# Cross attention on one core: bias products in three row groups, one GQA shift and exponential, separate softmax buffers, and new engine orders

## The chip, the cores and the metric

The kernel runs on one core of one Trainium2 chip. The time is that of the whole program on the device in microseconds. TensorE multiplies matrices, VectorE (DVE), ScalarE (ACT) and GpSimd (POOL) compute elementwise, SyncE (SP) issues the DMAs. Results of products land in PSUM, which here has eight banks of 512 float32 columns.

## The reference, cut to what matters

64 sequences `x` (128 tokens of width 128), each with a context of 77 tokens of width 256, pass through four cross attention layers. Layers 0 and 2 are grouped-query (GQA: 16 query heads of width 8, 4 key heads, RMS norm ahead), layers 1 and 3 are multi-head (MHA: 16 heads of width 64) with a bias on the score columns of four tokens.

```python
# layers 0 and 2
q = (rmsnorm(x, norm_w) @ wq).reshape(B, T, 16, 8)
k, v = [(cond @ w).reshape(B, S, 4, 8) for w in (wk, wv)]
attn = softmax(einsum('btgrd,bsgd->bgrts', qg, k) / sqrt(8))
x = x + einsum('bgrts,bsgd->btgrd', attn, v).reshape(B, T, 128) @ wo
# layers 1 and 3
logits = einsum('bhqd,bhkd->bhqk', x @ Wq, ctx @ Wk) / 8
col_bias[:, token_indices_A] = (-20 * (1 - mask_A))[:, None]
col_bias[:, token_indices_B] = (-20 * (1 - mask_B))[:, None]
probs = softmax(logits + col_bias)
x = x + einsum('bhqk,bhkd->bqhd', probs, ctx @ Wv) @ Wo + bo
```

## The kernel before

An item is one layer of one sequence. Eight sequences (streams) are under way at once, and `ITEMS` lists their 32 items so that GQA and MHA items alternate; `j` is an item's place. The loop body is `pair(it, n)`, written once for each engine: it handles GQA item g = 2n and MHA item m = 2n + 1, and, as a pipeline, parts of items before and after them (g + 2, g + 4, m - 2, m - 4, m - 6). The order of the calls in these five functions is the order of the engine's instructions; semaphores named after values tie the engines together, and `at(name, it, j, k)` gives the count to wait for. Pairs run 128 times, with some empty ones ahead (from n = -3, the fill) and behind (the tail).

Float32 accuracy is had from float16 products in three passes: a value is split into a high part (ScalarE, `high`) and a low part (VectorE `low`, or GpSimd `low_part`), and hi*hi, hi*lo, lo*hi are added in PSUM (`split_product`). For MHA, Wk and Wq are folded ahead of the loop into `m_w`; in the loop `folded` makes `g_s`, the keys seen from x, in six chunks for two streams at a time, three chunks a pair.

One item's scores are 16 heads x 77 keys = 1232 columns in `sc`, three PSUM banks of 512, 512 and 208 columns. Per MHA item, `scores_m(it, m, k)` fills bank k: first a bias product (L1350: `bias_l` times `bias_r`, both of 128 rows of which the first six are not zero), then three score products onto it (L1352). It waits for `sg_sub` or `sm_sub`, by which the shift of the item before has read the bank. Then `maximum_m` and `shift_m` on VectorE take the row maximum off into `shifted`, `exponential_m` on ScalarE writes `probs`, `high_m` and `low_part` split it into `p_sm`, and `turn_m` on SP transposes that by DMA into `p_tm`. `values_m` multiplies with the values, `normalise_m` and `normalise_rest` divide by the denominators, `high_out` and `low_out` split the result, `turn_out` transposes it, `output_m` multiplies with Wo, and `finish_m` adds the residual, or in layer 3 `last_layer` copies it to `y_out`, which `store` writes out. GQA items go the same way (`scores_g`, `maximum_g`, `shift_g` in two halves of 539 and 693 columns, `exponential_g` and `high_g` in two halves of 512 and 720, `values_g`, `normalise_g`, `rest_and_turn`, `turned`, `output_g`, `finish_g`); their keys are spread into `k_bd` by `spread_keys` on GpSimd, and their values are brought to packed form by `pick_values`, `picked_values` and `pack_values`. `probs` and `shifted` are one buffer each for both kinds; `item_before` says whose reading has to be over.

All other products take turns in `ring`, three PSUM banks. `ring_uses(n)` lists a pair's uses in TensorE's order, `bank_for` gives the bank and waits until the use three places before has been read.

`bias_factors` prepares `bias_l` and `bias_r` ahead of the loop on VectorE; each of its steps waits for the one before.

## Time and profile before

| | us |
|---|---|
| median of 3 runs | 1851.74 |
| lowest, highest | 1850.95, 1852.22 |
| profiled execution | 1852.7 |
| its span on the core | 1850.9 |
| TensorE busy in it | 1792.3 (97%) |
| VectorE, ScalarE, GpSimd busy | 1593.3 (86%), 1471.6 (80%), 1507.8 (81%) |
| TensorE's mean granted clock | 0.977 of full speed |

The page divides the span into 40 slices: TensorE stands at 9 tenths or more from the third to the last but one, and its granted clock at 9 tenths or more there too. A product's busy time covers its way through the array and into PSUM, so that successive products overlap in it; the cost of one in a stream is the distance from its start to the next start. In the timeline rows a group's first number is the start of its first instruction.

### The profile page before, as it was taken

The page shows a single profiled execution, that of the slowest core. Times are in us where ns is not written, and L with a number is a line of the kernel's source. Part 1 is how long each engine was busy: PE and PEld are TensorE (multiplying, and loading weights), DVE is VectorE, ACT ScalarE, POOL GpSimd, SP SyncE. Part 2 cuts the span into 40 slices and gives each one's busy share as a digit, 9 for nine tenths or more (in the row PEclk, how much of TensorE's full clock was granted, in tenths as well). Part 3 has the DMA queues.
Part 4 walks back from the last instruction along what each step waited for, and adds up shares of the span by engine and source line. Part 5 has one row for each costly group of instructions (what it writes and reads, how often), then busy time and mean ns, then how long its engine had stood idle before and what let it go on. Part 6 is the DMA issues. An engine that isn't in the chain of part 4 may idle for free.

```text
span 1850.9 us, 72762 instructions
## 1 busy us (share of the span) xinstructions
PE 1792.3 (97%) x28272; PEld 1557.7 (84%) x28272; DVE 1593.3 (86%) x3130; ACT 1471.6 (80%) x2859; POOL 1507.8 (81%) x1880
## 2 busy tenths in 40 slices
PE   6699999999999999999999999999999999999995
PEld 6578888888888888888888888888888888888884
DVE  6589988889888998898888998889888988889973
ACT  4378888888888888888888888888888888888872
POOL 3388888888888888888888888888888888888873
PEclk7599999999999999999999999999999999999998
DMA  5279999999999899999999999999899999989995
GB/s 170 42 140 183 167 187 183 184 182 166 178 192 180 181 168 184 185 173 188 175 180 187 177 175 178 182 190 177 176 178 186 185 173 177 169 176 178 177 165 128
DMA packets 1168210, 320.36 MB, mean 173 GB/s; under 512 B 1140246, under 2 KB 1164124, under 8 KB 1167868
## 3 DMA queue, kind: packets, MB, share of 16 engines
q1 hardware_dynamic: 1167868, 315.69, 93.1%
q8 instruction: 228, 3.74, 0.9%
q14 instruction: 114, 0.93, 0.2%
HBM read 15.93 MB, written 4.19 MB: 11 GB/s over the span
## 4 chain that ended last, share of the span: by engine, by line
PE 92%; issue 1%; DMA 0%; DVE 0%; POOL 0%; SPq 0%; ACT 0%
PE ring L1215 48%; PE sc L1352 11%; PE o_ps L1215 9%; PE o_ps L1370 5%; PE ring L1424 5%; PE sc L1335 4%; PE sc L1350 4%; PE ring L1286 2%; PE ring L1410 1%; PE ring L1405 1%; PE ring L1421 1%; PE sc L1327 1%; PE ring L1263 0%; PE o_ps L1366 0%; PE ring L1266 0%
## 5 line engine op out<-in xcount | busy, mean ns | idle before, releaser
L1215 PE MATMUL ring<-ctx_four,m_w 128*128 128x154 f16 x6144 | 441.4, 230 | 1.5 <-DVE v_tile L915 0.9
L1215 PEld LDWEIGHTS ring<-ctx_four,m_w 128*128 128x128 f16 x6144 | 422.8, 96 | 1.9 <-DVE v_tile L915 1.1
L636 POOL TENSOR_TENSOR p_sg<-arena,p_sg 128x512 f16<-128x512 f32 (+1 forms) x256 | 347.4, 1357 | 89.8 <-ACT p_sg L702 89.8
L1092 DVE TENSOR_TENSOR arena<-sc,row_max 128x616 f32<-128x616 f32 (+2 forms) x512 | 402.6, 797 | 13.2
L641 POOL TENSOR_TENSOR p_sm<-arena,p_sm 128x616 f16<-128x616 f32 x256 | 334.1, 1319 | 4.4 <-ACT p_sm L702 2.5
L664 POOL TENSOR_TENSOR arena<-arena 128x1024 f16<-128x1024 f32 x128 | 273.4, 2136 | 40.5 <-ACT arena L702 40.4
L702 ACT ACTIVATE arena<-ring 128x462 f16<-128x462 f32 (+1 forms) x384 | 198.3, 516 | 133.8 <-PE ring L1215 132.5
L1215 PE MATMUL ring<-wv_m,ctx_four 128*103 128x512 f16 (+1 forms) x1152 | 281.2, 380 | 0.6 <-DVE q_mix L919 0.6
L1071 DVE TENSOR_TENSOR arena<-ring,arena 128x462 f16<-128x462 f32 (+1 forms) x384 | 223.8, 584 | 64.2 <-ACT arena L702 55.4
L1352 PE MATMUL sc<-arena,x_s 128*128 128x512 f16 (+1 forms) x1152 | 262.2, 336 | 0.0
L1089 DVE TENSOR_REDUCE row_max<-sc 128x6 f32<-128x462 f32 (+2 forms) x384 | 223.7, 583 | 44.2 <-PE sc L1352 38.8
L812 ACT ACTIVATE arena<-arena,log_w,rstd 128x512 f32<-128x512 f32 (+1 forms) x256 | 228.3, 892 | 9.5 <-DVE arena L1092 9.5
L827 ACT ACTIVATE arena<-arena,log_w 128x616 f32<-128x616 f32 x256 | 204.0, 797 | 6.6 <-POOL p_sg L636 4.6
L702 ACT ACTIVATE v_tile<-ring 103x512 f16<-103x512 f32 (+1 forms) x192 | 114.9, 598 | 106.8 <-PE ring L1215 102.8
L1215 PEld LDWEIGHTS ring<-wv_m,ctx_four 128*103 128x103 f16 (+1 forms) x1152 | 136.3, 127 | 69.3 <-DVE q_mix L919 0.8
L702 ACT ACTIVATE p_sm<-arena 128x616 f16<-128x616 f32 x256 | 183.6, 717 | 6.1
L702 ACT ACTIVATE p_sg<-arena 128x512 f16<-128x512 f32 (+1 forms) x256 | 182.6, 713 | 4.1
L1084 DVE TENSOR_REDUCE row_max<-sc 128x16 f32<-128x1232 f32 x128 | 183.1, 1430 | 0.0
L1352 PEld LDWEIGHTS sc<-arena,x_s 128*128 128x128 f16 x1152 | 109.9, 97 | 76.3
L607 POOL TENSOR_TENSOR x_sq<-x_f 128x128 f32<-128x128 f32 x128 | 51.5, 402 | 146.6 <-ACT x_f L702 146.6
L915 DVE SCALAR_TENSOR_TENSOR v_tile<-ring,v_tile 103x512 f16<-103x512 f32 (+1 forms) x192 | 132.2, 689 | 40.9 <-ACT v_tile L702 40.9
L1141 DVE TENSOR_TENSOR arena<-o_ps,den_r 128x896 f32<-128x896 f32 x128 | 139.7, 1091 | 4.4
(165 smaller groups left out, 3797.4 us busy)
## 6 DMA issues: line engine op xcount, KB each, us to landing
v_fourth<-v_tile SPq DMA_DIRECT2D x64, 105.6 KB
ctx_nat<-in_ctx_dram SPq DMA_DIRECT2D x64, 77.0 KB
x_nat<-in_x_dram SPq DMA_DIRECT2D x64, 64.0 KB, 2.4
arena<-p_sg SPq DMA_TRANSPOSE x256, 3.9
arena<-p_sm SPq DMA_TRANSPOSE x256, 4.1
out_dram<-y_out SPq DMA_DIRECT2D x64, 64.0 KB, 2.1
v_fourth<-v_tile SPq DMA_DIRECT2D x32, 101.6 KB
arena<-in_L_xattn_Wk_dram SPq DMA_DIRECT2D x2, 1024.0 KB, 6.1
```

The lines of the kernel that those rows point to most:

```text
L636: pool.tensor_tensor(p_sg[k][:, LO, 0:e - a], probs_flat[:, a:e], p_sg[k][:, HI, 0:e - a], ALU.subtract).then_inc(sems["pg_lo"], 1)
L641: pool.tensor_tensor(p_sm[:, k, LO, :, 0:S], probs[:, hs, :], p_sm[:, k, HI, :, 0:S], ALU.subtract).then_inc(sems["pm_lo"], 1)
L664: pool.tensor_tensor(o_s[:, LO, :], o_n, o_s[:, HI, :], ALU.subtract).then_inc(sems["o_lo"], 1)
L702: return act.activation(out, in_, ACT.Copy, scale=scale)
L812: act.activation(probs_flat[:, a:e], shifted_flat[:, a:e], ACT.Exp, bias=log_w[:, :], scale=rstd[:, r:r + 1]).then_inc(sems["pg_exp"], 1)
L827: act.activation(probs[:, hs, :], shifted[:, hs, :], ACT.Exp, bias=log_w[:, :], scale=MHA_SCALE).then_inc(sems["pm_exp"], 1)
L1071: dve.tensor_tensor(both[LO], ring[:, b, 0:(h1 - h0) * 2 * S].rearrange("p (h t s) -> p h t s", t=2, s=S), both[HI], ALU.subtract).then_in ...
L1084: dve.tensor_reduce(row_max[:, :], s_view, AX_X, ALU.max).then_inc(sems["sg_max"], 1)
L1089: dve.tensor_reduce(row_max[:, h0:h1], s_view[:, h0:h1, :], AX_X, ALU.max).then_inc(sems["sm_max"], 1)
L1092: dve.tensor_tensor(shifted[:, hs, :], s_view[:, hs, :], row_max[:, hs].unsqueeze(2).to_broadcast([P, hs.stop - hs.start, S]), ALU.subtrac ...
L1215: ins = pe.matmul(out, a, b, start=(n == 0), stop=(n == len(passes) - 1))
L1352: ins = pe.matmul(sc_flat[:, a:e], x_s[st][:, x, :], g[:, y, a:e], start=False, stop=(x == LO))
```

## The change

- **Bias products.** `bias_factors` copies the six bias rows of `bias_l` and `bias_r` to partitions 32 and 64 too. `scores_m` issues all three bias products at k = 0, bank b from rows 32b to 32b + 5, and the score products follow; it waits once for both halves of the shift before.
- **GQA shift and exponential** are one operation each of 1232 columns. `high_g` keeps its two parts.
- **Buffers.** `probs_g`, `shifted_g`, `probs_m`, `shifted_m` replace `probs` and `shifted`; the waits go by item two places before, of the same kind. `x_sq` has three buffers and not eight.
- **Orders.** All five `pair` functions and `ring_uses` are written in a new order.

```diff
+        return [("vp", g - 2, 0), ("ot", g - 4, 0), ("g", lead, chunks[0]), ("ym", m - 6, 0), ("g", lead, chunks[1]),
+                ("kv", g + 2, 0), ("g", lead, chunks[2]), ("yg", g - 4, 0), *[("ct", g + 4, 0)] * (layer(g + 4) == 0 or n % PAIRS == CT_EXTRA), ("q", g + 2, 0),
+                *[("v", j, k) for j, k in value_chunks(n)[0:1]], *[("v", j, k) for j, k in value_chunks(n)[1:2]]]
...
-        probs = in_arena(HS, F32).rearrange("p (h s) -> p h s", s=S)
-        shifted = in_arena(HS, F32).rearrange("p (h s) -> p h s", s=S)
+        probs_g, shifted_g = in_arena(HS, F32), in_arena(HS, F32)
+        probs_m, shifted_m = [in_arena(HS, F32).rearrange("p (h s) -> p h s", s=S) for n in range(2)]
...
+                for k in range(1, 3):
+                    step(dve.tensor_copy(bias_l[32 * k:32 * k + 6, :], bias_l[0:6, :]))
+                    for n in range(2):
+                        step(dve.tensor_copy(bias_r[n][32 * k:32 * k + 6, :, :], bias_r[n][0:6, :, :]))
...
+            def shift_g(it, g):
                 dve.wait_ge(sems["sg_max"], at("sg_max", it, g, 1))
-                shifted_free(it, g, k)
-                shift(G_SUB[k], sems["sg_sub"])
+                if exists(it, g - 2):
+                    dve.wait_ge(sems["pg_exp"], at("pg_exp", it, g - 2, 1))
+                shift(shifted_g.rearrange("p (h s) -> p h s", s=S), slice(0, H), sems["sg_sub"])
...
-                scores_free(it, m, min(k, 1) + 1)
-                ind = bias_r[w][:, :, :].rearrange("p h s -> p (h s)")
                 a, e = k * BANK, min(HS, (k + 1) * BANK)
-                pe.matmul(sc_flat[:, a:e], bias_l[:, :], ind[:, a:e], start=True, stop=False)
+                if k == 0:
+
+                    scores_free(it, m, 2)
+                    ind = bias_r[w][:, :, :].rearrange("p h s -> p (h s)")
+                    for b in range(3):
+                        c0, c1, rows = b * BANK, min(HS, (b + 1) * BANK), slice(32 * b, 32 * b + 6)
+                        pe.matmul(sc_flat[:, c0:c1], bias_l[rows, :], ind[rows, c0:c1], start=True, stop=False)
```

The new order of TensorE is: `pick_values(g - 2)`, `values_m(m - 4)`, `rest_and_turn(g - 4)`, `scores_g(g)`, first folding chunk, `output_m(m - 6)`, second chunk, `keys_values(g + 2)`, third chunk, `scores_m` 0 and 1, `output_g(g - 4)`, `turn_inputs(g + 4)`, `queries(g + 2)`, `scores_m` 2, `values_g(g - 2)`, the context values. On GpSimd `spread_keys(g + 2)` now stands ahead of the low parts of item g; `pack_values` is a pair later and right behind `low_out`. On ScalarE `turned(g - 4)`, `high_out(m - 4)` and `last_layer(m - 6)` stand behind the first folding chunk, `keys_values` ahead of the exponential, `picked_values` behind the second value chunk. On SP both halves of `turn_m(m)` are in pair n, with `turn_out(m - 2)` behind them.

The three places below show what stands in a row on an engine. Behind each instruction are the semaphores that it waits for.

TensorE, in the middle of the run, from the keys and values of a GQA item (`wk_r`, `wv_g`) through the MHA scores (`sc<-arena,x_s`) to the last bank's scores; before:

```order
L1215 MATMUL ring<-wv_g,ctx_four 77x48 x6
L1350 MATMUL sc<-bias_r,bias_l 128x512 [waits sg_sub,g_lo,xm_lo]
L1352 MATMUL sc<-arena,x_s 128x512 x3
L1350 MATMUL sc<-bias_r,bias_l 128x512 [waits sg_sub,g_lo]
...
L1215 MATMUL ring<-x_s,wq_r 128x128 x11
L1350 MATMUL sc<-bias_r,bias_l 128x208 [waits sg_sub,g_lo]
L1352 MATMUL sc<-arena,x_s 128x208 x3
```

and after:

```order
L1206 MATMUL ring<-ctx_four,m_w 128x154 x11
L1345 MATMUL sc<-bias_r,bias_l 128x512 [waits sg_sub,g_lo,xm_lo]
L1345 MATMUL sc<-bias_r,bias_l 128x512
L1345 MATMUL sc<-bias_r,bias_l 128x208
L1347 MATMUL sc<-arena,x_s 128x512 x3
L1347 MATMUL sc<-arena,x_s 128x512 [waits g_lo]
L1347 MATMUL sc<-arena,x_s 128x512 x2
L1405 MATMUL ring<-o_tg,wo_g 128x128 [waits ot_copy,g_lo]
```

The second and third bias product moved up to the first, and the folding's last chunk (`m_w`) stands ahead of them where keys and values stood.

VectorE, around the GQA maximum (`row_max<-sc 128x16`) and shift, in the middle of the run; before:

```order
L1141 TENSOR_TENSOR arena<-o_ps,den_r 128x896 [waits om_rcp]
L1137 RECIPROCAL den_r<-ring 128x2 [waits om_norm,ot_raw,om_raw]
L1083 TENSOR_SCALAR ms<-sc 128x1 [waits sg_raw]
L1084 TENSOR_REDUCE row_max<-sc 128x16
L1092 TENSOR_TENSOR arena<-sc,row_max 128x539 [waits pm_exp,sg_max]
L1092 TENSOR_TENSOR arena<-sc,row_max 128x693 [waits pm_exp,sg_max]
```

and after:

```order
L1131 TENSOR_TENSOR arena<-o_ps,den_r 128x896 [waits om_rcp]
L1127 RECIPROCAL den_r<-ring 128x2 [waits om_norm,ot_raw,om_raw]
L1077 TENSOR_SCALAR ms<-sc 128x1 [waits sg_raw]
L1078 TENSOR_REDUCE row_max<-sc 128x16
L1065 TENSOR_TENSOR arena<-ring,arena 128x3x2x77 [waits g_hi]
L1086 TENSOR_TENSOR arena<-sc,row_max 128x1232 [waits pg_exp,sg_max]
L1065 TENSOR_TENSOR arena<-ring,arena 128x3x2x77 [waits g_hi]
```

The shift is one instruction and has a folding low part (L1065) ahead of it.

ScalarE, the last instructions of the program; `arena<-arena 128x1024` is `high_out`, `y_out` is `last_layer`, `arena<-ring,den_r` is `normalise_rest`; before:

```order
L702 ACTIVATE y_out<-ring 128x128 [waits stored5,ym_raw]
L702 ACTIVATE arena<-arena 128x1024 [waits turned_o,om_norm]
L745 ACTIVATE arena<-ring,den_r 128x64 [waits om_norm,om_rcp]
L745 ACTIVATE arena<-ring,den_r 128x64
L702 ACTIVATE y_out<-ring 128x128 [waits stored6,ym_raw]
...
L702 ACTIVATE y_out<-ring 128x128 [waits stored7,ym_raw]
```

and after:

```order
L698 ACTIVATE arena<-arena 128x1024 [waits turned_o,om_norm]
L698 ACTIVATE y_out<-ring 128x128 [waits stored5,ym_raw]
L741 ACTIVATE arena<-ring,den_r 128x64 [waits om_norm,om_rcp]
L741 ACTIVATE arena<-ring,den_r 128x64
...
L698 ACTIVATE y_out<-ring 128x128 [waits stored6,ym_raw]
L698 ACTIVATE y_out<-ring 128x128 [waits stored7,ym_raw]
```

Each `high_out` moved ahead of the `y_out` of the MHA item before.

## Rows read from the trace of the kernel before

**Rows 1.** Busy time by stretch: stretch, length, busy of each engine, PEclk, DMA share, GB/s

```profile
500.00:1000.00 500.00, 499.97 (x8067) 434.56 (x8067) 444.64 (x863) 417.54 (x817) 427.99 (x529) 1.00 0.99 181
1012.00:1015.00 3.00, 3.00 (x36) 2.21 (x35) 2.71 (x5) 2.55 (x4) 2.42 (x2) 1.00 1.27 280
```

**Rows 2.** TensorE's waits (us, times, longest): longest of 100 to 1800, one of the fill

```profile
PE ring L1215 <- DVE v_tile L915: 0.9, 1, 0.9
...
PE sc L1335 <- POOL k_bd L650: 6.0, 2, 3.4
```

**Rows 3.** Timeline of TensorE in one pair: start, us, engine, line, operation, count

```profile
1004.08 0.35 PE L1215 MATMUL ring<-v_tile,arena 128*128 128x65 f16 x6
...
1005.08 1.50 PE L1215 MATMUL ring<-arena,wo_m 128*128 128x128 f16 x24
1006.42 3.40 PE L1215 MATMUL ring<-ctx_four,m_w 128*128 128x154 f16 x48
1009.66 0.22 PE L1366 MATMUL o_ps<-zeros,arena 128*128 128x144 f16 x1
...
1010.48 0.38 PE L1215 MATMUL ring<-ctx_four,wk_r 128*128 128x77 f16 x6
...
1010.91 0.38 PE L1350 MATMUL sc<-bias_r,bias_l 128*128 128x512 bf16 x1
1011.13 0.81 PE L1352 MATMUL sc<-arena,x_s 128*128 128x512 f16 x3
```

**Rows 4.** Timeline of TensorE ahead of the loop, products of 64 rows

```profile
39.29 4.68 PE L1242 MATMUL sc<-arena 64*128 64x128 f32 x21
...
43.94 0.42 PE L1242 MATMUL ring<-arena 64*128 64x128 f32 x1
43.98 0.41 PE L1242 MATMUL sc<-arena 64*128 64x128 f32 x1
```

**Rows 5.** Groups by shape (busy us, mean ns): bias product, its weight load

```profile
L1350 PE MATMUL sc<-bias_r,bias_l 128*128 128x512 bf16 x256 | 96.9, 378 | 0.0
...
L1350 PEld LDWEIGHTS sc<-bias_r,bias_l 128*128 128x128 bf16 x384 | 38.0, 99 | 15.6
```

**Rows 6.** Timeline of VectorE in the pair of rows 3

```profile
1003.25 1.09 DVE L1141 TENSOR_TENSOR arena<-o_ps,den_r 128x896 f32<-128x896 f32 x1
...
1005.83 1.43 DVE L1084 TENSOR_REDUCE row_max<-sc 128x16 f32<-128x1232 f32 x1
...
1008.13 0.87 DVE L1092 TENSOR_TENSOR arena<-sc,row_max 128x693 f32<-128x693 f32 x1
1008.92 1.89 DVE L1071 TENSOR_TENSOR arena<-ring,arena 128x462 f16<-128x462 f32 x3
```

**Rows 7.** Timeline ahead of the loop: a bias_r copy, TensorE's first product of the loop

```profile
38.85 0.79 DVE L1003 CAST bias_r<-arena 6x1232 bf16<-6x1232 f32 x1
...
55.34 0.48 PE L1263 MATMUL ring<-ident,x_nat 128*128 128x128 f32 x1 [4.58 <-DVE m_w L915]
```

**Rows 8.** Timeline of the fill: the two operands of one item's scores

```profile
79.87 0.75 DVE L919 SCALAR_TENSOR_TENSOR q_mix<-q_hi,minus_low,ring 128x512 f16<-128x512 f16 x1 [2.32 <-ACT q_hi L702]
...
81.24 0.70 POOL L650 TENSOR_TENSOR k_bd<-k_mix,group_mask 128x308 f16<-128x308 f16 x1
```

**Rows 9.** Timeline of the tail: y_out, last rest product, both transposes, last high_out

```profile
1827.09 0.28 ACT L702 ACTIVATE y_out<-ring 128x128 f32<-128x128 f32 x1 [4.36 <-PE ring L1424]
...
1828.74 0.35 PE L1215 MATMUL ring<-v_fourth,arena 128*128 128x65 f16 x6
...
1830.69 1.58 SPq L518 DMA_TRANSPOSE arena<-arena  x1
...
1837.96 1.05 ACT L702 ACTIVATE arena<-arena 128x1024 f16<-128x1024 f32 x1
...
1841.41 1.51 SPq L518 DMA_TRANSPOSE arena<-arena  x1
```

More of the change, by code:

```diff
@@ L350, in build @@
         x_s = [sb(f"x_s{n}", [P, 2, T], F16) for n in range(STREAMS)]
-        x_sq = [sb(f"x_sq{n}", [P, T], F32) for n in range(STREAMS)]
+        x_sq = [sb(f"x_sq{n}", [P, T], F32) for n in range(3)] * 3
         y_out = [sb(f"y_out{n}", [P, D], F32) for n in range(STREAMS)]
@@ L544, in pair @@
                     turn_g(it, g, 1)
+                if exists(it, m - 2) and part(m - 2) != 3:
+                    move_values(it, m - 2)
                 if exists(it, m):
                     turn_m(it, m, 0)
+                    turn_m(it, m, 1)
+                if exists(it, m - 2):
+                    turn_out(it, m - 2)
                 if layer(g + 4) == 0 and exists(it, g + 4) and exists(it + 1, g + 4):
@@ L686, in pair @@
                 if exists(it, m):
-                    low_part(it, m, 0)
                     low_part(it, m, 1)
+                if layer(g + 4) == 0 and part(g + 4) == 3 and exists(it, g + 4):
+                    context_parts(it, g + 4)
             for n in range(-3, PAIRS):
@@ L1452, in pair @@
                     scores_m(it, m, 2)
+                if exists(it, g - 2):
+                    values_g(it, g - 2)
                 for j, k in value_chunks(n)[0:1]:
@@ L1475 @@
 CONSTS = 21
-ARENA = 15232
+ARENA = 16256
 SMALL_LOADS = 20
-DVE_STEPS = 73
+DVE_STEPS = 79
 _GQA = ("wq", "wk", "wv", "wo", "norm_w")
```

186 lines of the change are left out of this document (83 added, 103 removed).

## The prediction

> **What bounds the kernel now.** I read the busy table by stretches first. In the 500 us from 500 to 1000 TensorE is busy for 499.97 us at the full granted clock (1.00, the 2.4 GHz level), VectorE for 444.6, ScalarE for 417.5, GpSimd for 428.0 [rows 1]. A busy TensorE could still hide short waits, since the ends of its matmuls are modelled, so the waits of TensorE between 100 and 1800 us come next: the longest is 0.9 us, and there are three in all, 2.1 us together [rows 2]. In the middle of the run the time is therefore the sum of what TensorE issues, and only work taken off TensorE shortens it. The DMA share of 0.99 looks like a second ceiling but is none: in 3 us of backlog the same queue shows a share of 1.27 at 280 GB/s, against 181 GB/s on average [rows 1], so it has a third in hand. The ends of the run are different: there TensorE waits, 6.0 us of it in the fill for `k_bd` alone [rows 2].
>
> **The bias products.** Today each of the 128 MHA items issues three of them, in a chain with the score products. Starts in the timeline give their price: 1010.91 to 1011.13 is 0.22 us for one of 512 columns (there are two such) [rows 3], and the one of 208 is 0.09 at the same rate. Together 0.53 us an item. After the change the three stand in a row and read six rows each, at partitions 0, 32 and 64, into three different banks. Whether products in different row groups run at once is shown by the weight folding at the start, whose products have 64 rows and stand in one group or the other: 21 of them in a row last 4.68 us, the last one 0.41 of it, so they start 0.21 us apart, while where the groups alternate one starts at 43.94 and the next at 43.98 [rows 4]. So they do run side by side, and what is left is the longest, 0.22, and 0.01 to 0.04 for the later starts (0.04 is the gap of those rows; I take 0.01, since the second of a pair waits there for its own group): 0.23. Gross gain 0.30 us an item, 38 us in all.
>
> Against that stands what no row of the trace shows: the change from full-height products to six-row ones and back, twice an item. From below it costs nothing. From above, TensorE would let the pipeline run out and load weights in the open each time: a product of 512 columns lasts 0.378 us but its successor starts after 0.22, so 0.16 us of it is normally covered, and a weight load of that line lasts 0.10 [rows 5]. Twice 0.26 is 0.52 us an item, and the change would then lose 0.22 us. I take 0.11 us an item, a third of the two covered ends and no open load: waiting for the array alone is a part of those 0.16 us (the rest is reading and writing), and nearly every weight load of the trace lies under other work. That leaves 0.19 us an item, **minus 24.3 us**. Here the Trainium skill speaks against the change: its page "TensorEngine Tiling (Array Packing)", section "Key Properties", says that changing the tiling mode drains TensorE. No row of this trace shows it. Its page "TensorE: Matmul & The Clock Gate", section "Measured speedup vs the span model", gives 3.07 times for four row groups at 512 columns, which as an estimate from that page is some 280 ns a set and a gain of some 0.25 us an item, or 32 us, if the switches are in it.
>
> **The new order in the middle.** No work is added to TensorE, so the order costs something only if a producer becomes late. The tightest place is the first bias product: it writes all three banks, so it now waits for the whole GQA shift, and the shift is one operation. From the last score product of the GQA item (end near 1005.08) to the first of the MHA item TensorE issues the output product (1005.08 to 1006.42), the folding (to 1009.66) and keys and values (1010.48 to 1010.91), 1.34 + 3.24 + 0.43 = 5.01 us [rows 3]; `values_g`, which stood there too, moves behind and takes 0.82 us of cover with it. VectorE has to do in that time the maximum 1.43, one folding low part (a third of 1.89), a short residual sum (0.3 at most) and the shift, now 128x1232 (0.87 for 693 columns, so 1.5) [rows 6]: 3.9 us. Ahead of that it has `normalise_m`, 1.09 and two short reciprocals, about 1.5 us, which waits for `values_m`; that ends 1.0 us before the scores do (1004.08 to 1005.08, the small rest product and the scores) [rows 3], so VectorE comes some 0.5 us late. 0.5 + 3.9 = 4.4 against 5.0: 0.6 us in hand. The second tight place is the `ot` bank, freed by ScalarE's `turned` behind its first folding copy: two short copies under the output product's 1.34 us, with some 0.4 in hand. `values_m`, although the code now names m - 4, stands at nearly the same place of the stream, so the transposes keep the cover they have. Work on the other engines shrinks a little (one shift and one exponential in place of two), and separate buffers only take waits away. GpSimd's `low_out` stands ahead of `pack_values` now, and `values_g` is late enough for it. I put **0** for all this; what it costs if the cover is gone is the second rival. Two small exceptions are at the ends.
>
> **The start.** `bias_factors` gets six more copies, each waited for. VectorE is busy without a gap there, and TensorE's first product of the loop at 55.34 waits 4.58 us for VectorE's last weight part [rows 7], so they count in full. A copy of 6x1232 from float32 took 0.79 [rows 7]; four from bf16 at 0.4 to 0.8 and two narrow ones at 0.25: 2.1 to 3.7, **plus 2.9**.
>
> **The fill.** `spread_keys` leaves its place behind both low parts on GpSimd. The second `k_bd` came at 81.24 + 0.70 = 81.94, while the other operand of the same scores, `q_mix`, was there at 79.87 + 0.75 = 80.62 [rows 8]. What is late next is `q_mix`, which also loses the copy of the picked values ahead of it (0.5 us on ScalarE). So of the 6.0 us about half comes back: **minus 3** (bounds 0 and minus 6).
>
> **The tail.** Before, ScalarE's `high_out` of an item stands behind the last copy `y_out` of the item before: high_out of the last item starts at 1837.96, right behind that copy, and after GpSimd's low part its transpose goes out at 1841.41, 3.45 us on [rows 9]. After, `high_out` stands ahead of `y_out`, and the transpose waits only for the output product of the item before, its single buffer. For the last but one item that was over when y_out began at 1827.09; its transpose went out at 1830.69 [rows 9], so it comes 3.6 us sooner. Its output product, over before 1837.96, is then over before 1834.4. The last item's own values end at 1828.74 + 0.35 = 1829.1 [rows 9]; normalising takes about 1.6 and the rest on ScalarE 0.5, and 3.45 more bring 1834.6. The last transpose leaves there and not at 1841.41: **minus 7** (bounds minus 3 and minus 9, as the clock falls here and there).
>
> **The sum.** Minus 24.3 + 2.9 - 3 - 7 = minus 31.4 us. The profiled execution took 1852.7 us (span 1850.9), 1 us over the median of 1851.7, so 1821.3 by its own time and **1820.5** as a median. A measurement of this kernel can tell about 0.2%, 3.7 us, from no change.
>
> **The rivals.** First, the slower side: **the switches cost more than the side by side run saves**. It decides at 0.30 us an item from where the bias products stop paying, and at 0.30 + 7.1/128 = 0.36 from where the kernel is slower; at the full 0.52 the bias alone adds 28 us and the time is 1852.7 + 28 - 7 - 1 = 1873. For it speaks that this stream never lets TensorE run dry and six-row products come in the middle of it; against it, that three quarters or more of both open ends would have to be paid. I give 0.10. The page on tiling named above would be right about the drain in either case; only its size decides.
>
> Second, **the new order starves TensorE**: the shift of 1232 columns, or `ot_copy`, is late by more than the 0.4 to 0.6 us in hand, in every pair. Each 0.1 us of it costs 12.8 us, 0.24 us eat the whole gain, and a stall of 0.3 us gives 1821 + 38 = 1859. For it: VectorE is 89% busy [rows 1], and the chain through it is now a closed one of few steps. Against it: the 11% left over are more than it needs, and it waits for TensorE in each pair, so that it can't fall behind slowly. Chance 0.09.
>
> Third, **the three products don't overlap**, for instance because their weight loads or starts follow one another: the bias stays at 0.53 us and only the ends pay, 1852.7 - 7 - 1 = 1844.6. The alternating starts of [rows 4] speak against it. Chance 0.06.
>
> **How the numbers follow.** The forecast, with its bias gain between 0 and 38 us, has 0.75. Its ends are 1852.7 - 38 - 1 - 7 - 5 = 1802 (full overlap, free switches, a better fill and tail) and about 1847. The range reaches from 1802 to 1851: it takes in the third rival and leaves out the first two for the most part and 0.03 below, 0.17 in all. Faster by over 0.2% (below 1848): 0.75 + 0.06, less the thin upper end and plus the mild cases of the first two, 0.82. Within 0.2%: 0.05. Slower: 0.13.
>
> **What would show it.** In the profile after, the starts of the first bias product and of the score product behind it should lie 0.30 to 0.38 us apart, where 0.53 went in three pieces before; 0.23 means free switches, 0.53 or more the first or third rival, and the starts of the three tell which (a few ns apart or 0.2 us). A full-height product just ahead of the first would show the switch in. TensorE's waits from 100 to 1800 should stay near 2 us; a line `sc <- DVE` on the bias line or `ring <- ACT o_tg` with over a hundred entries is the second rival. The first product of the loop should start near 58 in place of 55.34, the `k_bd` line should lose most of its 6.0 us, and the last two output products should start about 7 us apart, not 11. I would be wrong most likely in the price of the switch, next in the ends.

## The result: two thirds of the bias products' gain is paid back in changes of height

The changed kernel took **1838.8 us** in the median (1836.3 to 1839.6, 4 runs) beside 1852.0 (1851.0 to 1853.3) for the kernel before on the same chip: ratio 0.9926, 95% interval 0.9909 to 0.9943. Measured again (experiment 9), it gave 1837.9 (1837.3 to 1840.1) against 1854.3, ratio 0.9915 (0.9901 to 0.9928). So it is faster by 13.2 to 16.5 us, where 31 were forecast: the sign and the range held, the size was about twice too large. Three executions at a lower mean granted clock (0.65 to 0.84) are left out of all medians: 2538.3 and 2024.3 us of the kernel before, and 2211.8 us of experiment 2. The profiled execution took 1836.3 us (span 1834.5), the fastest of its four; against the profiled one of before it is 16.4 us shorter.

First, is TensorE still what bounds the middle? The busy table of that stretch (stretch, length, busy of TensorE, its weight loads, VectorE, ScalarE, GpSimd, then the granted clock, DMA share, GB/s), answering to [rows 1]:

```profile
500.00:1000.00 500.00, 500.00 (x8116) 430.32 (x8114) 442.11 (x831) 402.53 (x783) 427.86 (x532) 1.00 0.98 182
```

And its waits from 100 to 1785 us (total, times, longest), then three of those between 55 and 110 us, answering to [rows 2]:

```profile
PE ring L1206 <- ACT o_tg L698: 1.6, 2, 0.8
PE ring L1206 <- DVE v_tile L905: 0.3, 1, 0.3
```

```profile
PE ring L1254 <- DVE m_w L905: 6.8, 1, 6.8
PE ring L1254 <- DVE v_gqa L905: 6.2, 3, 2.6
PE sc L1326 <- DVE q_mix L909: 2.0, 2, 1.2
```

In the middle nothing is waited for: the same full clock, 1.9 us of waits in all. There the time is still the sum of what TensorE issues, and whatever is missing of the gain lies in TensorE's own stream. In the fill the `k_bd` line of [rows 2] is gone, but others have come. The timeline of TensorE around one MHA item's first scores (start, us, line, operation, count), answering to [rows 3]:

```profile
1004.28 0.38 PE L1206 MATMUL ring<-wv_g,ctx_four 128*77 128x48 f16 x6
1004.50 0.97 PE L1206 MATMUL ring<-ctx_four,m_w 128*128 128x154 f16 x12
1005.41 0.39 PE L1345 MATMUL sc<-bias_r,bias_l 6*128 6x512 bf16 x3
1005.73 1.47 PE L1347 MATMUL sc<-arena,x_s 128*128 128x512 f16 x6
1007.03 0.38 PE L1405 MATMUL ring<-o_tg,wo_g 128*128 128x128 f32 x2
```

The three bias products last 0.39 us together, one product's length: they do run at once. From the first's start to the score product is 1005.73 - 1005.41 = 0.32 us. Single products at the same place show what the group's row hides, the distance in front of it. TensorE's products, then the loads of the bias weights, then the score products behind the first:

```profile
1005.25 0.23 PE L1206 MATMUL ring<-ctx_four,m_w 128*128 128x154 f16 x1
1005.41 0.39 PE L1345 MATMUL sc<-bias_r,bias_l 6*128 6x512 bf16 x3
1005.73 0.39 PE L1347 MATMUL sc<-arena,x_s 128*128 128x512 f16 x1
```

```profile
1005.40 0.10 PEld L1345 LDWEIGHTS sc<-bias_r,bias_l 6*128 6x128 bf16 x3
```

```profile
1005.96 0.59 PE L1347 MATMUL sc<-arena,x_s 128*128 128x512 f16 x2
```

The last folding product starts at 1005.25 and the bias at 1005.41, 0.16 us on, where folding products otherwise start 0.067 apart. The bias weights are loaded at 1005.40, only then. The profile's modelled end of the folding product is 1005.48, behind the bias start, so the row says when the next product may start and not what TensorE does meanwhile. From the starts in the trace in ns, alike within 2 ns for all items between the ninth and the fourth last pair, one item's bias was and is:

| distance of starts, ns | before | after |
|---|---|---|
| last product before the group, to the bias | as ever (38 to 67) | 161, of which 67 as ever: +94 |
| the bias products | 216 + 216 + 89 = 521 | 3 + 3 + 314 = 320 |
| first score product, to the second | 216 | 226: +10 |
| bias and its changes of height | 521 | 424 |

(The entries are rounded; the mean of the last row after is 425.) That is 97 ns less an item, 12.4 us for 128. The forecast had 190 ns, 24.3 us. To see where all of it went, the run is cut into three stretches. The mark is the start of a GQA item's first product (`sc<-ones,x_sq`, L1318): first item, ninth item, the 116 pairs from the ninth to the fourth last, and from there to the last product's start. All are profiled executions, us:

| kernel | first item at | ninth at | 116 pairs | end |
|---|---|---|---|---|
| before | 60.3 | 160.7 | 1576.4 | 111.2 |
| after | 63.2 | 161.5 | 1566.1 | 104.2 |
| after, full height (1) | 60.8 | 160.0 | 1577.0 | 105.8 |
| before, side by side (2) | 62.7 | 161.8 | 1568.6 | 110.1 |
| after, one row group (3) | 63.3 | 165.5 | 1601.0 | 107.3 |
| before, swap (4) | 60.2 | 159.6 | 1578.6 | 106.4 |
| after, three places (5) | 63.3 | 167.6 | 1649.2 | 109.5 |
| after, two halves (6) | 62.1 | 160.6 | 1576.2 | 106.1 |
| after, late copies (7, 10) | 61.0, 61.1 | 161.4, 159.7 | 1566.3, 1566.9 | 104.4, 104.8 |
| after, no bias (8) | 63.3 | 159.7 | 1520.0 | 102.5 |
| after again (9) | 63.3 | 161.7 | 1566.1 | 105.0 |
| after, swap undone (11) | 63.3 | 162.0 | 1566.1 | 108.7 |
| before, three parts (12) | 60.5 | 160.7 | 1569.0 | 106.4 |

From before to after: +0.8 to the ninth item, -10.3 in the middle, -7.0 at the end. The outer stretches scatter between executions of one kernel: the ninth item by 1.7 us (7 and 10), the end by 0.8 (after, 104.2, and 9, 105.0). Of the 128 MHA items, 5 have their first scores ahead of the ninth GQA item and 7 in the end.

The start and the fill, VectorE and TensorE, answering to [rows 7] and [rows 8]:

```profile
44.39 0.98 DVE L1009 COPY bias_r<-bias_r 6x1232 bf16<-6x1232 bf16 x2
...
57.77 0.47 PE L1254 MATMUL ring<-ident,x_nat 128*128 128x128 f32 x1 [6.78 <-DVE m_w L905]
...
82.05 0.70 POOL L646 TENSOR_TENSOR k_bd<-k_mix,group_mask 128x308 f16<-128x308 f16 x1
82.47 0.75 DVE L909 SCALAR_TENSOR_TENSOR q_mix<-q_hi,minus_low,ring 128x512 f16<-128x512 f16 x1
...
83.28 0.56 PE L1277 MATMUL ring<-v_gqa,picks 128*128 128x36 f16 x10 [1.43 <-DVE q_mix L909]
...
84.20 1.19 PE L1326 MATMUL sc<-k_bd,q_mix 128*128 128x308 f16 x6
```

The copies cost 57.77 - 55.34 = 2.4 us. `k_bd` is no longer last. But the scores of that item begin at 84.20, and less those 2.4 us that is 81.8, where they could begin at 81.94 before [rows 8]. TensorE's product of the picked values, which in the new order stands between the queries and the scores, waits for the ring bank that `q_mix` frees at 83.22, and it and the short products behind it take the next 0.9 us. A wait on another engine's step has taken the place of the one removed, at nearly the same time.

The end, ScalarE and SyncE's queue, answering to [rows 9]:

```profile
1816.48 0.28 ACT L698 ACTIVATE y_out<-ring 128x128 f32<-128x128 f32 x1 [2.01 <-PE ring L1419]
1821.08 0.52 ACT L741 ACTIVATE arena<-ring,den_r 128x64 f32<-128x64 f32 x2 [4.32 <-DVE den_r L1127]
1821.63 1.06 ACT L698 ACTIVATE arena<-arena 128x1024 f16<-128x1024 f32 x1
1824.20 0.28 ACT L698 ACTIVATE y_out<-ring 128x128 f32<-128x128 f32 x1 [1.51 <-PE ring L1419]
```

```profile
1816.85 1.83 SPq L515 DMA_TRANSPOSE arena<-arena  x1
...
1825.06 1.56 SPq L515 DMA_TRANSPOSE arena<-arena  x1
```

The last `high_out` (1821.63) now stands ahead of the copy `y_out` and follows the item's own normalising at once; its transpose leaves 8.2 us after the one before, not 10.7 [rows 9].

### The profile page after: what moved, and what is told of

It reads as the page before. It is cut to its first block, busy times and chain, and to the rows that moved or that the text cites. A ratio compares the mean times of both kernels' runs of the same rounds, so it can differ in the third digit from the quotient of the medians.

```text
span 1834.5 us, 71998 instructions
## 1 busy us (share of the span) xinstructions
PE 1780.1 (97%) x28272; PEld 1533.7 (84%) x28272; DVE 1580.0 (86%) x3008; ACT 1411.3 (77%) x2731; POOL 1496.6 (82%) x1880
## 4 chain that ended last, share of the span: by engine, by line
PE 94%; DVE 3%; issue 1%; POOL 1%; ACT 1%; SPq 0%; DMA 0%; ACTq 0%; POOLq 0%
PE ring L1206 50%; PE sc L1347 12%; PE o_ps L1206 9%; PE o_ps L1365 5%; PE ring L1419 5%; PE sc L1326 4%; PE ring L1277 2%; PE ring L1405 2%; PE sc L1345 1%; PE ring L1400 1%; PE ring L1416 1%; PE sc L1318 1%; DVE m_w L905 1%; PE ring L1257 0%; PE o_ps L1361 0%
## 5 line engine op out<-in xcount | busy, mean ns | idle before, releaser
L1206 PE MATMUL ring<-ctx_four,m_w 128*128 128x154 f16 x6144 | 480.6, 229 | 3.6 <-ACT o_tg L698 3.3
L1206 PEld LDWEIGHTS ring<-ctx_four,m_w 128*128 128x128 f16 x6144 | 427.7, 96 | 4.6 <-ACT o_tg L698 4.0
L1086 DVE TENSOR_TENSOR arena<-sc,row_max 128x616 f32<-128x616 f32 (+1 forms) x384 | 385.1, 1003 | 0.5 <-issue 0.2
L632 POOL TENSOR_TENSOR p_sg<-arena,p_sg 128x512 f16<-128x512 f32 (+1 forms) x256 | 342.1, 1357 | 2.4 <-ACT p_sg L698 2.4
L1065 DVE TENSOR_TENSOR arena<-ring,arena 128x462 f16<-128x462 f32 (+1 forms) x384 | 225.1, 586 | 87.7 <-ACT arena L698 78.5
L1206 PE MATMUL ring<-wv_m,ctx_four 128*103 128x512 f16 (+1 forms) x1152 | 272.1, 381 | 0.5 <-DVE x_f L1137 0.5
L1347 PE MATMUL sc<-arena,x_s 128*128 128x512 f16 (+1 forms) x1152 | 243.0, 338 | 0.0
L801 ACT ACTIVATE arena<-arena,log_w,rstd 128x1232 f32<-128x1232 f32 x128 | 179.4, 1402 | 4.0 <-DVE arena L1086 2.0
L698 ACT ACTIVATE p_sg<-arena 128x512 f16<-128x512 f32 (+1 forms) x256 | 175.8, 711 | 4.1
L1347 PEld LDWEIGHTS sc<-arena,x_s 128*128 128x128 f16 x1152 | 95.9, 98 | 89.4 <-issue 28.6
```

The source lines that it names most:

```text
L632: pool.tensor_tensor(p_sg[k][:, LO, 0:e - a], probs_g[:, a:e], p_sg[k][:, HI, 0:e - a], ALU.subtract).then_inc(sems["pg_lo"], 1)
L698: return act.activation(out, in_, ACT.Copy, scale=scale)
L801: act.activation(probs_g, shifted_g, ACT.Exp, bias=log_w[:, :], scale=rstd[:, r:r + 1]).then_inc(sems["pg_exp"], 1)
L1065: dve.tensor_tensor(both[LO], ring[:, b, 0:(h1 - h0) * 2 * S].rearrange("p (h t s) -> p h t s", t=2, s=S), both[HI], ALU.subtract).then_in ...
L1086: dve.tensor_tensor(out, s_view[:, hs, :], row_max[:, hs].unsqueeze(2).to_broadcast([P, hs.stop - hs.start, S]), ALU.subtract).then_inc(do ...
L1206: ins = pe.matmul(out, a, b, start=(n == 0), stop=(n == len(passes) - 1))
```

## The experiments

The theory (A): a change of the products' height, into six rows and back, costs about 0.10 us each time, and eats most of what the three products save side by side. The rivals: the products don't really run at once, or save less; the new orders cost something in the middle. There are twelve runs; the kernel before, measured beside each, took 1853.2 us (experiments 1 to 4), 1853.2 (5 to 8) and 1854.3 (9 to 12).

**1. After, with full-height bias products in a row, and no copies.**

```diff
-                        c0, c1, rows = b * BANK, min(HS, (b + 1) * BANK), slice(32 * b, 32 * b + 6)
-                        pe.matmul(sc_flat[:, c0:c1], bias_l[rows, :], ind[rows, c0:c1], start=True, stop=False)
+                        c0, c1 = b * BANK, min(HS, (b + 1) * BANK)
+                        pe.matmul(sc_flat[:, c0:c1], bias_l[:, :], ind[:, c0:c1], start=True, stop=False)
```

> The kernel after the change, with the three bias products at full height again (128 rows of bias_l and bias_r), still in a row ahead of the score products, and without the six copies ahead of the loop. Theory A (each change of height costs TensorE some 0.10 us, so that side by side saves only about 0.095 us an item, 12 us in all, and the new orders are about neutral in the middle): some 10 us slower than the changed kernel, 1845 to 1849. Theory B (side by side saves the 24 us that were forecast and the new orders lose 11 of them in the middle): 1838.8 + 24 - 2, some 1861, slower than the kernel before.

Measured: 1847.4 us (1846.9 to 1849.1), ratio to before 0.9973 (0.9961 to 0.9985). TensorE's products at the place (of the three bias products one has no record):

```profile
1009.49 0.30 PE L1202 MATMUL ring<-ctx_four,m_w 128*128 128x154 f16 x2
1009.84 0.47 PE L1341 MATMUL sc<-bias_r,bias_l 128*128 128x512 bf16 x2
1010.15 0.59 PE L1343 MATMUL sc<-arena,x_s 128*128 128x512 f16 x2
```

No gap: the last folding product and the second bias product start 67 + 216 = 283 ns apart in the trace, and the score products 216. Side by side is worth (1577.0 - 1566.1) / 116 = 94 ns an item in the middle. The bias factors are bf16 here too, beside float16 products, so the gap doesn't come from the type. Everything else of the change together (orders, one shift, buffers) brought 0.7 us to the ninth item, cost 0.6 in the middle and brought 5.4 at the end; the first of these is less than the scatter, the other two agree with the median, 5.8 us below the kernel before.

**2. Before, with the bias products side by side and the copies, nothing else.**

```diff
-                scores_free(it, m, min(k, 1) + 1)
...
-                pe.matmul(sc_flat[:, a:e], bias_l[:, :], ind[:, a:e], start=True, stop=False)
+                if k == 0:
...
+                    scores_free(it, m, 2)
...
+                    for b in range(3):
+                        c0, c1, rows = b * BANK, min(HS, (b + 1) * BANK), slice(32 * b, 32 * b + 6)
+                        pe.matmul(sc_flat[:, c0:c1], bias_l[rows, :], ind[rows, c0:c1], start=True, stop=False)
```

> The kernel before, with only the bias products side by side in three row groups ahead of the first score product, and the six copies. Theory A: 12 us saved, 2 us given back by the copies, 1842. Theory B: 24 saved, 2 given back, 1830. A third possibility is that the wait for both halves of the GQA shift costs time in the old order; then a wait of TensorE on a VectorE shift shows in each pair, and the time is near 1852 or above.

Measured: 1845.2 us (1844.6 to 1845.6), ratio 0.9958 (0.9941 to 0.9974), 3 us short of A's 1842. The gaps are those of the changed kernel: the 48-column product ahead of the group is followed after 128 ns and not 38, the group takes 320 ns, the first score product 227. That saves some 11.4 us in the 116 pairs by these starts, and 7.8 are left. The rest is in waits that the kernel before doesn't have, from 165 to 1750 us (total, times, longest):

```profile
PE ring L1429 <- issue: 1.0, 1, 1.0
PE ring L1219 <- DMA arena<-arena: 0.8, 1, 0.8
PE o_ps L1378 <- DMA arena<-p_sg: 0.3, 1, 0.3
```

With shorter ones beside them, starts there are late by 3.1 us in all, five of them by 0.2 to 1.2 us each, where the kernel before has one, of 0.2. I read that as TensorE, once faster, running into what is behind it in the old order; no run tests this.

**3. After, with all three in rows 0 to 5.**

```diff
-                        c0, c1, rows = b * BANK, min(HS, (b + 1) * BANK), slice(32 * b, 32 * b + 6)
+                        c0, c1, rows = b * BANK, min(HS, (b + 1) * BANK), slice(0, 6)
```

> The kernel after the change, with all three six-row products in rows 0 to 5, so in one row group. Theory A: they follow one another, 0.22 + 0.22 + 0.09, and only two changes of height an item are paid: 0.30 us an item or 38 us more than the changed kernel, 1877. If the price sits in the small products themselves and not in the change of height, each would start later than 0.22 us after the one before, and the time is above 1885.

Measured: 1877.4 us (1876.1 to 1878.4), ratio 1.0131 (1.0116 to 1.0146), what A said to 0.4 us. TensorE's products in three narrow stretches, the folding product ahead, the three bias products and the score product:

```profile
1027.93 0.23 PE L1206 MATMUL ring<-ctx_four,m_w 128*128 128x154 f16 x1
1028.09 0.60 PE L1345 MATMUL sc<-bias_r,bias_l 6*128 6x512 bf16 x2
```

```profile
1028.32 0.37 PE L1345 MATMUL sc<-bias_r,bias_l 6*128 6x512 bf16 x1
```

```profile
1028.53 0.25 PE L1345 MATMUL sc<-bias_r,bias_l 6*128 6x208 bf16 x1
1028.71 0.39 PE L1347 MATMUL sc<-arena,x_s 128*128 128x512 f16 x1
```

The starts lie 161, 226, 216 and 180 ns apart: six-row products on the same rows run one after the other, so the row groups are what makes them run at once. Against experiment 1, which differs only in the height, the middle is longer by (1601.0 - 1577.0) / 116 = **207 ns an item for two changes**. The trace in ns has them as 94 (161 for 67) and 10 (226 for 216) on the way in, 91 (180 for 89) and 10 (the first score product's 226 for 216) on the way out.

**4. Before, with ScalarE's `high_out` ahead of `last_layer`.**

```diff
-                if layer(m - 4) == LAYERS - 1 and exists(it, m - 4):
-                    last_layer(it, n + 1, m - 4)
                 if exists(it, m - 2):
                     high_out(it, m - 2)
+                if layer(m - 4) == LAYERS - 1 and exists(it, m - 4):
+                    last_layer(it, n + 1, m - 4)
```

> The kernel before, with ScalarE's high_out(m - 2) ahead of last_layer(m - 4) and nothing else. Theory of the tail (the chain y_out, high_out, low part, transpose, output product is what spaces the last items by 10.7 us): the last two output products start some 7 us apart, and the time is 1845. Rival (another wait takes its place, the single o_t or the clock's fall): no change, 1852, or half of it.

Measured: 1849.1 us (1848.5 to 1850.3), ratio 0.9979 (0.9969 to 0.9988): 4.1 us. The expected 1845 was missed; about half of the gain came, as the rival allowed, and the last two output products start 8.8 us apart, not 7. ScalarE near the end:

```profile
1833.67 0.52 ACT L745 ACTIVATE arena<-ring,den_r 128x64 f32<-128x64 f32 x2 [7.49 <-DVE den_r L1137]
1834.22 1.06 ACT L702 ACTIVATE arena<-arena 128x1024 f16<-128x1024 f32 x1
1836.15 0.28 ACT L702 ACTIVATE y_out<-ring 128x128 f32<-128x128 f32 x1 [0.87 <-PE ring L1424]
```

`high_out` starts 3.7 us sooner than the 1837.96 of [rows 9], right behind the normalising of its own item, which is now the last to come: it waits for the item's values, and these for the transposes of its probabilities. The end is 4.8 us shorter, the middle 2.2 longer, with starts up to 1.0 us late, as in experiment 2.

**5. After, with the six-row products at three places.**

```diff
-                    for b in range(3):
-                        c0, c1, rows = b * BANK, min(HS, (b + 1) * BANK), slice(32 * b, 32 * b + 6)
-                        pe.matmul(sc_flat[:, c0:c1], bias_l[rows, :], ind[rows, c0:c1], start=True, stop=False)
...
+                pe.matmul(sc_flat[:, a:e], bias_l[0:6, :], ind[0:6, a:e], start=True, stop=False)
```

> The changed kernel, but the three six-row products are not side by side: each, from rows 0 to 5, stands ahead of the score products of its own bank, as in the kernel before. That makes six changes of height in an item where the changed kernel and the run with all three in one row group have two. Theory A (each change of height costs the same, about 0.10 us: 90 ns of gap and, with a full bank behind it, 11 ns on the first product after it): four changes more than the run in one row group, 4 x 0.10 = 0.40 us/item less some 10 to 20 ns for the narrow bank, over 128 items 49 to 52 us: 1877 + 50 = 1927 (1922 to 1931). Theory B (the price belongs to the first product of a group whose operands are cold, or is paid once for an item, not for each change): close to the run in one row group, 1877 to 1885. Theory C (the gap is the end of a short product that can't be covered, and behind a 512-column product there is none): two of the four new gaps vanish or more, 1877 to 1905.

Measured: 1929.3 us (1927.5 to 1930.9), ratio 1.0410 (1.0395 to 1.0426). B and C fall. Four changes more than in experiment 3 are (1649.2 - 1601.0) / 116 = 416 ns, **104 ns each**. Behind 512-column products the gap is no smaller; the last two score products of a bank, the bias product, and the score product behind it:

```profile
1012.65 0.59 PE L1344 MATMUL sc<-arena,x_s 128*128 128x512 f16 x2
1013.18 0.38 PE L1342 MATMUL sc<-bias_r,bias_l 6*128 6x512 bf16 x1
```

```profile
1013.49 0.39 PE L1344 MATMUL sc<-arena,x_s 128*128 128x512 f16 x1
```

The score products start at 1012.65 and 1012.86 (0.22 on), the bias at 1013.18: 312 ns behind the last one for 216, and 317 to the next score product.

**6. After, with 64 rows to a product in two halves.**

```diff
-                        c0, c1, rows = b * BANK, min(HS, (b + 1) * BANK), slice(32 * b, 32 * b + 6)
+                        c0, c1, rows = b * BANK, min(HS, (b + 1) * BANK), slice(64 * (b % 2), 64 * (b % 2) + 64)
...
```

> The changed kernel with 64 rows to a product in place of six: the first and the third bias product in rows 0 to 63, the second in rows 64 to 127, side by side with them; rows without a factor hold zeros. Only one copy of the factors is made at the start (three copies fewer, about 1.2 us less). The third product (208 columns, 88 ns) now follows the first on the same rows, so the group is 0.09 us/item longer: +11.3 us. Theory A (a change of height costs the same between full height and 64 rows as between full height and six): 1838.8 + 11.3 - 1.2 = 1849 (1846 to 1852). Theory B (halves cost less than a small group, say half of the 0.20 us): 1836. Theory C (products in two halves do not run at once): the group's first two products in a row, 216 ns more: 1876.

Measured: 1848.2 us (1847.4 to 1849.6), ratio 0.9975 (0.9965 to 0.9984), as A said:

```profile
1009.79 0.23 PE L1205 MATMUL ring<-ctx_four,m_w 128*128 128x154 f16 x1
1009.95 0.39 PE L1344 MATMUL sc<-bias_r,bias_l 64*128 64x512 bf16 x2
```

```profile
1010.18 0.25 PE L1344 MATMUL sc<-bias_r,bias_l 64*128 64x208 bf16 x1
1010.36 0.39 PE L1346 MATMUL sc<-arena,x_s 128*128 128x512 f16 x1
```

The first two start 3 ns apart, the third 223 ns later on the first's rows, and both gaps (0.16 in front, 182 for 89 ns behind) are those of the six-row group. So what is paid for is the change, not how small the group is.

**7 and 10. After, with late and narrow copies**, twice; the second time beside **9, the changed kernel once more**.

```diff
-                for k in range(1, 3):
-                    step(dve.tensor_copy(bias_l[32 * k:32 * k + 6, :], bias_l[0:6, :]))
-                    for n in range(2):
-                        step(dve.tensor_copy(bias_r[n][32 * k:32 * k + 6, :, :], bias_r[n][0:6, :, :]))
...
             split_out(1)
             fold_low(1)
+            for k in range(1, 3):
+                c0, c1, band = k * BANK, min(HS, (k + 1) * BANK), slice(32 * k, 32 * k + 6)
+                step(dve.tensor_copy(bias_l[band, :], bias_l[0:6, :]))
+                for n in range(2):
+                    ind = bias_r[n][:, :, :].rearrange("p h s -> p (h s)")
+                    step(dve.tensor_copy(ind[band, c0:c1], ind[0:6, c0:c1]))
...
-            pe.wait_ge(dve_step, DVE_STEPS)
+            pe.wait_ge(dve_step, DVE_STEPS - 6)
...
+                    if it == 0 and m == 1:
+                        pe.wait_ge(dve_step, DVE_STEPS)
```

> The changed kernel, with the six copies of the factors written behind the last preparation on VectorE instead of ahead of the GQA weights, each copy only of the columns that its product reads, and TensorE's wait for them moved from the start of its loop to the first bias product. Theory A (the copies delay the chain that ends with the last part of m_w by 2.4 us, and all of it reaches the end, as the full-height run without copies starts its first item 2.4 us earlier): 1838.8 - 2.4 = 1836.4 (1835.5 to 1837.5). Theory B (the delay is swallowed in part while the pipeline fills: the ninth GQA item is only 1.5 us earlier without the copies): 1837.3. Theory C (VectorE has no room behind the last preparation, so the first items wait instead): 1838 to 1840, no gain.

Measured: 1836.2 us (1834.7 to 1838.3), 2.6 below the changed kernel's first 1838.8. But the ranges touch, and in its profile the 2.2 us of the first item were gone by the ninth, so it was run again beside the changed kernel.

> The changed kernel once more, unedited, so that the next run can be compared with it on one chip. The same as before by both theories: 1838.8 (1836 to 1840).

> The kernel with late and narrow copies once more, beside the changed kernel. Its first GQA item began 2.2 us earlier, but in the profiled execution of each the fourth began at the same time (95.7 and 95.9 us), and the clock rose at about 86 us in the changed kernel's and at about 89 us in the other's. Theory A (the 2.2 us reach the end, and the moment at which the clock rises is scatter of one execution): 2.0 to 2.8 us below the changed kernel, 1836.3. Theory B (an earlier start brings no earlier rise of the clock, so the fill swallows it): within 0.5 us of the changed kernel.

Measured: the changed kernel 1837.9 (1837.3 to 1840.1), with late copies **1835.6 (1834.7 to 1836.0)**, ratio to before 0.9897 (0.9884 to 0.9911). The ranges don't touch: 2.2 us, and A holds. Why the first profile hid it is in the busy table from 86 to 88 us (the granted clock is the third number from the end), of the first run (7) and of the second (10):

```profile
86.00:88.00 2.00, 1.66 (x14) 1.67 (x15) 1.85 (x2) 0.28 (x2) 0.00 (x0) 0.50 0.99 232
```

```profile
86.00:88.00 2.00, 1.77 (x32) 1.77 (x33) 1.96 (x2) 0.52 (x3) 0.00 (x0) 1.00 0.80 195
```

TensorE's clock, at 0.50 of full speed (1.2 GHz) since the loop began, rises to 1.00 (2.4 GHz) before 86 us in the one execution and only after 88 in the other. The ninth item then starts at 159.7 or at 161.4 us. That is scatter between executions of one kernel, of the size of the effect. The late copies on VectorE in the second run take the time in which it would be idle ahead of `ctx_four`:

```profile
54.62 0.68 DVE L905 SCALAR_TENSOR_TENSOR m_w<-o_ps,m_w 128x512 f16<-128x512 f32 x1
55.32 0.18 DVE L1038 COPY bias_l<-bias_l 6x128 bf16<-6x128 bf16 x1
55.54 0.60 DVE L1041 COPY bias_r<-bias_r 6x512 bf16<-6x512 bf16 x2
...
57.05 0.32 DVE L905 SCALAR_TENSOR_TENSOR ctx_four<-ring,ctx_four 128x154 f16<-128x154 f32 x1
```

**8. After, without the bias products** (the bias of the MHA scores is left out of what is computed).

> The changed kernel without the bias products: the bias of the MHA scores is left out of what is computed, and the first score product of each bank starts the sum. It prices the whole group as it now stands, and shows whether TensorE is still the bound without it. In the changed kernel the group holds TensorE from 158 ns after the last m_w product to 321 ns after its own first start, against 67 ns: 0.41 us/item, and 11 ns on the first score product: 0.42 us/item, 128 items: 54 us. Theory A (TensorE stays the bound): 1838.8 - 54 = 1785 (1782 to 1789). Theory B (the other engines take over before that): the gain stops short, 1795 to 1825, with waits of TensorE in the middle of the run in place of none.

Measured: 1788.8 us (1786.8 to 1790.2), ratio 0.9651 (0.9637 to 0.9666): 50 us for the whole group, 4 short of A. It lies at the upper end of A's 1782 to 1789. In the middle 397 ns an item are gone where the starts give 425; TensorE's waits from 165 to 1750 us have grown, on the transposed probabilities above all:

```profile
PE o_ps L1206 <- DMA arena<-p_sm: 2.2, 5, 0.7
```

So TensorE stays the bound, and the next one, the transposes, begins to show some 50 us below.

**11. After, with the swap on ScalarE undone.**

```diff
-                if exists(it, m - 4):
-                    high_out(it, m - 4)
                 if layer(m - 6) == LAYERS - 1 and exists(it, m - 6):
                     last_layer(it, n, m - 6)
+                if exists(it, m - 4):
+                    high_out(it, m - 4)
```

> The changed kernel with ScalarE's two steps at the end of an item swapped back: an item's last layer (the rounding of its output for the last projection) stands ahead of the other item's rounding of the normalised head outputs, as in the kernel before. Theory A (this swap is what shortens the end: in the kernel before, made alone, it took 4.8 us off the end and left 3.9 in the median): 3.5 to 5 us slower than the changed kernel, 1842.3 to 1843.8, with the stretch from the start of the fourth last GQA item to the last product at 109 to 111 us against 104.2. Theory B (all of the 7 us of the end come from the swap): 1845 to 1846. Theory C (the rest of the new order brings them): no difference.

Measured: 1841.2 us (1840.9 to 1843.9), 3.3 slower than the changed kernel beside it, end 108.7 against 105.0. ScalarE shows the copy ahead of `high_out` again:

```profile
1826.45 0.28 ACT L698 ACTIVATE y_out<-ring 128x128 f32<-128x128 f32 x1 [2.49 <-PE ring L1419]
1826.63 1.05 ACT L698 ACTIVATE arena<-arena 128x1024 f16<-128x1024 f32 x1
```

It lies just under A's 3.5 to 5. Of the 6 to 7 us of the end the swap is worth 3.3 to 4.8; the rest comes with the new order, and which part of it wasn't taken apart.

**12. Before, with three parts alone**: side by side, the swap of experiment 4, the late and narrow copies of 7. Its diff is those of 2, 4 and 7 together.

> The kernel before with three things alone: the products side by side, ScalarE's swap, and the late and narrow copies; its orders, its shared buffers and its shift and exponential in two are kept. Theory A (the gains add, and the new orders bring little beyond the swap): 1853.2 - 7.8 (side by side as measured in this order, copies and all) - 3.9 (swap) - 2.3 (copies) = 1839.2 (1837 to 1841). Theory B (the waits of TensorE that came up in the middle with each of the two alone, 2 to 3 us in 1568, grow when both are made, since TensorE now gains on the engines behind it in the old order): 1842 to 1846.

Measured: 1839.0 us (1836.1 to 1841.6), ratio 0.9918 (0.9905 to 0.9930). A holds: three small edits in the old order reach the changed kernel. The new orders and buffers are still worth 3.4 us, since with the same copies they give 1835.6 (its highest run, 1836.0, just below the lowest here, 1836.1). By the table 2.1 of it are in the middle and 1.6 at the end; the profiled pair is 4.7 us apart, with another 1.0 ahead of the ninth item, within its scatter. The waits of the middle stay small here (0.6, 0.3 and 0.3 us); by the starts, six products behind a GQA item's scores come up to 0.6 us late.

## Why the prediction was right and wrong

- **What bounds the kernel** was right: no wait in the middle, and in the new order every ns taken off TensorE's stream there reached the end until experiment 8 took 50 us. In the old order it did not quite: experiment 2 kept 7.8 of 11.4 us in the middle.
- **Gross gain of the bias products**, 0.30 us an item, was right: with free changes the group would be 3 + 3 + 213 = 219 ns, 302 less than 521. The starts lie 3 ns apart where I took 10.
- **The step that failed is the price of the change of height**: "I take 0.11 us an item, a third of the two covered ends and no open load". Measured are 205 ns an item by the rounded starts and 207 between experiments 1 and 3: 94 + 10 in, 91 + 10 out. The gap is nearly six tenths of the 0.16 us that I had called covered, at both ends, and not a third. The load of 0.10 us does not add to it (the product starts 4 ns after its load), so 0.52 was far off as well. Over 128 items the term is minus 12.4 us and not minus 24.3; this is 12 of the 15 us by which the profiled time missed the sum.
- **The sign that I named was blind on one side.** "0.30 to 0.38 us apart" came true with 0.32, and would have passed for a right forecast. It holds only the way out; the way in lies in front of the first bias product.
- **The first rival** had its deciding points right (0.30 and 0.36 us an item); at 0.21 it is not reached. The page "TensorEngine Tiling (Array Packing)" of the Trainium skill, section "Key Properties", says that changing the mode drains TensorE. The trace agrees so far as each change costs a gap of some 93 ns; whether that is the emptying of the array or a fixed time of switching, no run separates. The estimate from "TensorE: Matmul & The Clock Gate", section "Measured speedup vs the span model", 0.25 us an item, was too good by 0.15: whatever its 3.07 times holds, it isn't two changes of height inside a full-height stream.
- **The third rival** (no overlap) fell: starts 3 ns apart, and one row group is 39 us slower.
- **The second rival** (the order starves TensorE) did not come: 1.9 us of waits. Zero for the order in the middle was nearly right; it costs 0.6 us by experiment 1. By the starts, the next product comes 10 ns an item later behind the context values (`wv_m`) and behind `ident_y`'s products, and 16 ns sooner behind `x_nat`'s, with smaller differences elsewhere.
- **The start**, plus 2.9: 2.4. **The fill**, minus 3: minus 0.7 by experiment 1, within the 1.7 us by which the ninth item scatters. I asked what is late next and named `q_mix`, rightly, but took its time as the time of the scores, as in the kernel before, where nothing stands between the two. In TensorE's new order the product that waits for `q_mix`'s bank does, with what follows it. The wait that was to give 3 us gave 0.2 at this item.
- **The tail**, minus 7: minus 7.0 in one execution and 6.1 in the other (experiment 9), of which the bias products of its seven items give 0.7 and the named cause some 4. That the number came out is in part luck; the output products are 8.0 and 8.3 us apart, not 7.

The terms as measured: - 12.4 (bias, all items) + 0.6 (middle) + 2.4 - 0.7 - 6.3 (the end's 7.0 without the 0.7 of its bias products) = - 16.4, as between the two profiled executions; the medians give - 13.2 and - 16.5. The exact agreement is luck, since the fill scatters by 1.7 us and the end by 0.8; why the two pairs of medians differ by 3 us, no run shows.

## What to carry to other kernels

Products with few rows can run at once in row groups, but in a stream of full-height products each visit costs 0.21 us for the two changes: at this clock a group pays only if it saves about one whole product of 512 columns (0.22 us), so gather the small products at one place (four changes more an item cost 52 us). When a chip behaviour has no row in the trace, make the sign to look for cover the whole term, the distance before the first instruction as well as the one behind the last. And when an order is changed to remove a wait, ask of the new order, engine by engine, what stands between the next late operand and its use.

## What the runs showed of the hardware

- A change of TensorE's height costs 90 to 96 ns of gap, and the first product behind it holds the next one off by 10 ns more than usual, at the full granted clock. It is the same into six rows, into 64 rows and back, and behind products of 48, 77, 128, 154 and 512 columns (38 to 128, 66 to 160, 56 to 152, 67 to 161 and 216 to 312 ns).
- At a change, the weights are loaded only at its end, 4 ns ahead of the product; otherwise they are loaded while the product ahead streams. The second load behind the change starts 11 ns after the product, and not 2, which goes with the 10 ns; why, no run shows. All of this is at the full granted clock: no bias product ran at the lower level.
- Products in different row groups, at partitions 0, 32 and 64 or 0 and 64, start 3 ns apart, and on the same rows 216 ns (512 columns), however few rows they read.
- A copy of 6x1232 bf16 on VectorE took 0.49 us (0.98 for two), against 0.79 from float32 [rows 7].
- TensorE's granted clock rose from 0.50 to 1.00 at 85.1 us in one execution and at 89.8 us in another of the same kernel (experiments 10 and 7), and the ninth item came at 159.7 and 161.4 us. Differences of 2 us need several runs here, and one profile doesn't settle them.
